# Attention's input in a Macaron block: both expert rows of a token summed by VectorE, the output bias summed later on GpSimd

## The chip, the cores and the metric

One core of one Trainium2 chip runs the kernel. The metric is device microseconds of one execution. Before the change three runs took 290.08, 288.76 and 292.3 us (median 290.08); one more execution was profiled.

## The reference, cut to what matters

The block is half an expert layer, attention, and half an expert layer again, each on a layer-normalised input and added to the residual x (4 sequences of 256 tokens, 512 channels, fp32):

```
def ffn(x):                                   # 8 experts, top 2, biases b_gate and b_e
    _, top_idx = top_k(x @ W_gate + b_gate, 2)
    y_all = relu(einsum('bsd,edh->bseh', x, W_e) + b_e)
    return take_along_axis(y_all, top_idx[..., None], axis=2).mean(axis=2)
def attn(x):                                  # one head of 128
    q, k, v = split(x @ Wqkv + bqkv)
    return softmax(q @ k.T / sqrt(128)) @ v @ Wo + bo
x = x + 0.5 * ffn(layernorm(x))
x = x + attn(layernorm(x))
x = x + 0.5 * ffn(layernorm(x))
```

What attention reads is therefore x plus two rows per token, one from each of its experts, already scaled by 0.25 (0.5 for the half layer, 0.5 for the mean). The output bias bo is added to x as well.

## The kernel before, in words

The 1024 tokens are 8 tiles of 128 (one token per partition, 512 channels along it). A batch is one sequence, so two tiles: batch b has tiles 2b and 2b+1. The tensor `x` holds all 8 tiles in SBUF and is updated in place.

In an expert layer tokens are sorted by expert into 23 tiles; GpSimd gathers their rows from HBM by indirect DMA, TensorE multiplies, and GpSimd scatters the results to `z_dram`, upper and lower row of each token apart. Attention then loads these rows back into `z_rows`, a ring of two slots (ZB = 2), each with both rows of one tile: `z[:, 0, :]` and `z[:, 1, :]`. Batch 0's four rows are loaded one by one (L376); tiles 2 to 7 come with one DMA each (L379), issued by SP when the tile two places ahead has been summed into x (semaphore `x_ffn`).

Every engine has its own program, written out by hand, and carries it out in that order; semaphores are the only tie between engines. Attention runs batch by batch:

- **VectorE** adds z to x (`add_z_batch`, L1167, with `add_z`, L1158), takes mean and variance (`moments`, L940), and, when GpSimd has made the reciprocal root (`deviations`, L435, instruction L442), normalises both tiles (`normalise`, L969, instruction L978, tensor `xn`). It also adds v's bias (L1176), takes the row maximum of the scores (L1218) and scales it to `nmax` (L1219), and adds attention's output to x (L1244), which also needs bo in x (semaphore `bo_added`).
- **GpSimd** sums, for tiles 2 to 7, both rows of z into the first (`sum_z`, L473, instruction L477, semaphore `z_summed`), so that VectorE adds one tensor per tile (L1165). For tiles 0 and 1 VectorE adds the rows one after the other (L1204 and L1162). GpSimd also adds bo to each tile of x, as soon as that tile is normalised (`add_bo`, L479, instruction L482).
- **TensorE** transposes xn (L698), projects to q and k (L822), then to v (L831), makes the scores (L840), transposes the probabilities (L848), mixes v (L856) and projects out (L866). Within batch b it also makes the transposes, q, k and v of batch b+1, and from batch 1 on the transposes ("g1") and the gate of the second expert layer for batch b-1.
- **ScalarE** copies results out of PSUM and takes the exponentials.

`norms` lists the order in which tiles are normalised, for attention ("att") and for the second layer ("g1"); `norm_no` is a tile's place in it and the count in the semaphore `xn_made`.

Of the kernel before, what the change touches and what calls it, by code (L numbers as in the profile page):

```python
# [6 lines left out]
ALU = mybir.AluOpType  # L7
# [11 lines left out]
def macaron_kernel(nc, x_in, w_qkv, b_qkv, w_o, b_o, w_gate, b_gate, w_e, b_e, out):  # L19
# [12 lines left out]

    B, S, H = x_in.shape
    E, _, HO = w_e.shape
    D = w_o.shape[0]
    T = B * S
    NT = T // P
    NC = H // P
    TB = S // P
# [17 lines left out]
    with ExitStack() as ctx:  # L57
        def sb(name, shape, dt=F32, at=ctx):
            return at.enter_context(nc.sbuf_tensor(name, shape, dt))
# [4 lines left out]
        def sem(name):  # L64
            return ctx.enter_context(nc.semaphore(name))
# [9 lines left out]
        ZB = 2  # L75
        MR = 8
        x = sb("x", [P, NT, H])
# [89 lines left out]
        def z_slot(i):  # L167

            return z_rows[:, i % ZB, :, :]
# [35 lines left out]
        dve_step = sem("dve_step")  # L205
# [3 lines left out]
        xn_made = sem("xn_made")  # L209
# [24 lines left out]
        z_in = [sem(f"z_loaded{s}") for s in range(ZB)]  # L234
        z_half_in = [[sem(f"z_half_loaded{k}_{i}") for i in range(NT // 2)] for k in range(TOP_K)]
        lower_added = sem("lower_added")
        z_first = [[sem(f"z_first{i}_{k}") for k in range(TOP_K)] for i in range(TB)]
        z_summed = sem("z_summed")
        x_ffn = sem("x_ffn")
        bo_added = sem("bo_added")  # L240
        qk_done = sem("qk_done")
# [28 lines left out]
        norm_no = {u: n for n, u in enumerate(norms)}  # L270
# [123 lines left out]
        def _(pool):  # L394
# [40 lines left out]
            def deviations(kind, b):  # L435

                n = norm_no[(kind, TB * b)]
                s = n % MR
                pool.wait_ge(var_made, n // TB + 1)
                if n >= MR:  # L440
                    pool.wait_ge(xn_made, n - MR + TB)
                pool.tensor_tensor(rstd[:, s:s + TB], var_eps[:, s:s + TB], neg_half[:], ALU.pow  # L442
                                   ).then_inc(rstd_made, 1)
# [26 lines left out]
                        gather(f, t + XG + 1)  # L470
                    scatter(f, t)

            def sum_z(i):  # L473

                pool.wait_ge(z_in[i % ZB], 16 * (i // ZB))
                z = z_slot(i)
                pool.tensor_tensor(z[:, 0, :], z[:, 0, :], z[:, 1, :], ALU.add).then_inc(z_summed, 1)  # L477

            def add_bo(b):  # L479
                for i in range(TB * b, TB * (b + 1)):  # L480
                    pool.wait_ge(xn_made, norm_no[("att", i)] + 1)
                    pool.tensor_tensor(x[:, i, :], x[:, i, :], bo_bc[:], ALU.add).then_inc(bo_added, 1)  # L482

            def attention_input(b):
                for i in range(TB * b, TB * (b + 1)):
                    sum_z(i)
                deviations("att", b)

            for b in range(B):
                deviations("g0", b)  # L490
            experts(0)
            pool.wait_ge(att_in, 16 * ATT_LOADS)
            deviations("att", 0)
            pool.wait_ge(xn_made, norm_no[("att", TB - 1)] + 1)
            attention_input(1)
            add_bo(0)
            add_bo(1)
            for b in range(B):
                if b + 2 < B:
                    for i in range(TB * (b + 2), TB * (b + 3)):  # L500
                        sum_z(i)
                if b:
                    deviations("g1", b - 1)
                if b + 2 < B:
                    deviations("att", b + 2)
                    add_bo(b + 2)
            deviations("g1", B - 1)
            experts(1)

# [417 lines left out]
        def _(dve):  # L927
            steps = [0]

            def step(ins):  # L930

                steps[0] += 1
                ins.then_inc(dve_step, 1)
                return steps[0]
# [5 lines left out]
            def moments(kind, b):  # L940

                n = norm_no[(kind, TB * b)]
                s = n % MR
                read = []
                for i in range(TB):
                    if kind == "g0":
                        dve.wait_ge(x_in_sem[TB * b + i], 16)
                    if (kind, b) == ("att", 0):
                        add_z(i)
                        dve.wait_ge(x_ffn, i + 1)  # L950
                    read.append(step(dve.bn_stats(stats[:, s + i, :], x[:, TB * b + i, :])))
                for i in range(TB):
                    dve.wait_ge(dve_step, read[i])
                    last = step(dve.bn_aggr(mv[:, s + i, :], stats[:, s + i, :]))
                dve.wait_ge(dve_step, last)
                if n >= MR:
                    dve.wait_ge(rstd_made, (n - MR) // TB + 1)
                dve.tensor_scalar(var_eps[:, s:s + TB], mv[:, s:s + TB, 1], EPS, None,  # L958
                                  ALU.add).then_inc(var_made, 1)
# [197 lines left out]

            def add_z(i):  # L1158

                if i < TB:  # L1160
                    dve.wait_ge(z_first[i][1], 16)
                    dve.tensor_tensor(x[:, i, :], x[:, i, :], z_slot(i)[:, 1, :], ALU.add).then_inc(x_ffn, 1)  # L1162
                else:
                    dve.wait_ge(z_summed, i - TB + 1)
                    dve.tensor_tensor(x[:, i, :], x[:, i, :], z_slot(i)[:, 0, :], ALU.add).then_inc(x_ffn, 1)  # L1165

            def add_z_batch(b):  # L1167
                for i in range(TB * b, TB * (b + 1)):
                    add_z(i)
                dve.wait_ge(x_ffn, TB * (b + 1))  # L1170

            def add_bv(b):
# [32 lines left out]
            moments("att", 0)  # L1205
            normalise("att", 0)
            add_z_batch(1)
            moments("att", 1)
            normalise("att", 1)
# [4 lines left out]
            for b in range(B):  # L1214
# [8 lines left out]
                if b + 2 < B:  # L1223
                    add_z_batch(b + 2)
# [15 lines left out]
                for q in range(TB):  # L1240
                    i = TB * b + q
# [48 lines left out]
```

## Time and profile before

| | us |
|---|---|
| median of three runs (288.76 to 292.3) | 290.08 |
| the profiled execution | 285.84 |
| its span, from first to last instruction | 284.0 |
| TensorE busy (PE; its weight loads, PEld, lie beside it) | 242.9 (86%) |
| VectorE busy (DVE) | 168.1 (59%) |
| GpSimd busy (POOL) | 127.6 (45%) |
| ScalarE busy (ACT) | 102.8 (36%) |
| GpSimd's sums of z (L477), 6 | 7.5 |
| GpSimd's sums of the bias (L482), 8 | 10.8 |
| VectorE's sums of z for tiles 2 to 7 (L1165), 6 | 6.0 |

Times within the execution count from the start of the span. Attention lies at about 121 to 178 us. "Busy" is the time in which an engine carries out instructions; idle time in front of an instruction is listed with what ended it. A granted clock of 1.00 is 2.4 GHz, 0.50 is 1.2 GHz.

### The profile page before, as it was taken

How to read it: one execution, taken by the hardware profiler on the slowest of the kernel's cores; microseconds unless marked ns; L12 is line 12 of the kernel's file. 1: busy time of each engine (PE TensorE's matmuls, PEld its weight loads, DVE VectorE, ACT ScalarE, POOL GpSimd, SP SyncE). 2: the span in 40 equal slices, each digit the busy share in tenths (PEclk: the TensorE clock that was granted, in tenths of full speed). 3: DMA queues.
4: the chain of work that ended last, by engine and by line, in shares of the span. 5: the costliest groups of instructions: out<-in, count | busy, mean ns of one | idle time of the engine just before them, and what ended most of it. 6: DMA issues, size and time to landing. Idle time of an engine off the chain costs nothing. (4 is left out here: it accounts for less than half of the span.)

```text
span 284.0 us, 4851 instructions
## 1 busy us (share of the span) xinstructions
PE 242.9 (86%) x1298; PEld 178.7 (63%) x1299; DVE 168.1 (59%) x404; ACT 102.8 (36%) x183; POOL 127.6 (45%) x141
## 2 busy tenths in 40 slices
PE   6677698989999999987999967559999999999730
PEld 2343266668888887566686934326888888887520
DVE  4589948976343444576888568872434344344770
ACT  1987425553333433112343442201343333333200
POOL 4200455765666563349464000024556666555150
PEclk9999999999999999999999999559999999999995
DMA  7999259993444365412401021104445434359891
GB/s 244 387 393 395 102 158 379 413 342 122 145 159 151 117 180 180 148 54 96 147 4 74 0 77 74 75 7 144 144 139 165 162 124 158 112 160 307 293 376 43
DMA packets 22787, 49.35 MB, mean 174 GB/s; under 512 B 4332, under 2 KB 4972, under 8 KB 22512
## 3 DMA queue, kind: packets, MB, share of 16 engines
q1 hardware_dynamic: 13712, 26.55, 25.9%
q0 software_dynamic: 7360, 20.46, 21.9%
q10 hardware_dynamic: 1696, 2.11, 2.0%
q8 instruction: 9, 0.15, 0.2%
q14 instruction: 10, 0.08, 0.1%
HBM read 34.42 MB, written 18.35 MB: 186 GB/s over the span
## 5 line engine op out<-in xcount | busy, mean ns | idle before, releaser
L457 POOL DMA_INDIRECT z_dram<-yrow,place x46 | 51.2, 1113 | 59.9 <-ACT yrow L587 42.1
L449 POOL DMA_INDIRECT xg<-xn_dram,tok x46 | 47.3, 1028 | 49.3 <-DVE tok L1109 32.9
L1120 DVE TENSOR_TENSOR xt_lo<-tp_ps,xt_hi 128x512 fp32r<-128x512 f32 x46 | 31.8, 691 | 56.1 <-ACT xt_hi L577 53.2
L587 ACT ACTIVATE yrow<-ypre 128x512 f32<-128x512 f32 x42 | 26.5, 632 | 84.7 <-DVE ypre L1128 46.5
L577 ACT ACTIVATE xt_hi<-tp_ps 128x512 fp32r<-128x512 f32 x46 | 26.8, 582 | 15.3 <-PE tp_ps L759 15.3
L759 PE MATMUL tp_ps<-ident,xg 128*128 128x128 f32 x184 | 27.9, 274 | 3.5 <-DMA xg<-xn_dram,tok 3.4
L782 PE MATMUL y_ps<-whi,xt_hi 128*128 x96 | 29.1, 425 | 1.7 <-ACT xt_hi L577 1.1
L759 PEld LDWEIGHTS tp_ps<-ident,xg 128*128 128x128 f32 x184 | 22.4, 140 | 11.4 <-DMA xg<-xn_dram,tok 6.1
L782 PE MATMUL qk_ps<-whi,xt_hi 128*128 x88 | 26.7, 425 | 0.6 <-issue 0.5
L782 PE MATMUL y_ps<-whi,xt_lo 128*128 x96 | 26.5, 398 | 0.0
L782 PE MATMUL y_ps<-wlo,xt_hi 128*128 x96 | 26.1, 393 | 0.0
L442 POOL TENSOR_TENSOR rstd<-var_eps,neg_half 128x2 f32<-128x2 f32 x12 | 8.4, 700 | 35.6 <-DVE var_eps L958 35.6
L782 PE MATMUL qk_ps<-whi,xt_lo 128*128 x88 | 24.1, 396 | 0.0
L782 PE MATMUL qk_ps<-wlo,xt_hi 128*128 x88 | 23.9, 393 | 0.0
L1128 DVE TENSOR_TENSOR ypre<-y_ps,be_bc 128x512 f32<-128x512 f32 x22 | 15.2, 691 | 11.8 <-PE y_ps L782 10.4
L685 PE MATMUL rk_ps<-ones 128*128 128x512 bf16 x63 | 19.3, 462 | 2.3 <-POOL neg_half L411 2.3
L782 PEld LDWEIGHTS y_ps<-wlo,xt_hi 128*128 128x128 f32 x96 | 18.1, 188 | 4.3
L782 PEld LDWEIGHTS y_ps<-whi,xt_hi 128*128 128x128 f32 x96 | 16.5, 190 | 6.4 <-issue 4.3
L782 PEld LDWEIGHTS y_ps<-whi,xt_lo 128*128 128x128 f32 x96 | 18.0, 189 | 4.1
L1128 DVE TENSOR_TENSOR ypre<-qk_ps,be_bc 128x512 f32<-128x512 f32 x20 | 13.8, 692 | 10.2 <-PE qk_ps L782 8.7
L305 DVE TENSOR_TENSOR wlo<-raw,whi 128x1024 fp32r<-128x1024 f32 x16 | 19.0, 1216 | 0.5 <-ACT whi L520 0.5
L782 PEld LDWEIGHTS qk_ps<-whi,xt_lo 128*128 128x128 f32 x88 | 16.6, 189 | 3.9
(130 smaller groups left out, 350.3 us busy)
## 6 DMA issues: line engine op xcount, KB each, us to landing
raw<-in_L_ffn_W_e_dram SPq DMA_DIRECT2D x16, 512.0 KB, 9.2
z_rows<-z_dram SPq DMA_DIRECT2D x6, 512.0 KB, 3.3
x<-in_L_attn_x_dram SPq DMA_DIRECT2D x8, 256.0 KB, 3.9
be_bc<-in_L_ffn_b_e_dram SPq DMA_DIRECT2D x2, 1024.0 KB, 12.6
xn_dram<-xn ACTq DMA_DIRECT2D x8, 256.0 KB, 2.0
whi<-z_dram SPq DMA_DIRECT2D x4, 512.0 KB, 4.6
wlo<-z_dram SPq DMA_DIRECT2D x4, 512.0 KB, 6.4
out_dram<-x SPq DMA_DIRECT2D x8, 256.0 KB, 2.8
```

The costliest lines, as they stand in the source:

```text
L305: eng.tensor_tensor(half(wlo, n), half(raw, n), half(whi, n).bitcast(F32), ALU.subtract).then_inc(done, 1)
L442: pool.tensor_tensor(rstd[:, s:s + TB], var_eps[:, s:s + TB], neg_half[:], ALU.pow).then_inc(rstd_made, 1)
L449: pool.indirect_dma_start(out=xg[:, t % XG, :], out_offset=None, in_=xn_dram[f][:, :], in_offset=bass.IndirectOffsetOnAxis(ap=tok[:, t:t + ...
L457: pool.indirect_dma_start(out=z_dram[f][:, :], out_offset=bass.IndirectOffsetOnAxis(ap=place[:, t:t + 1], axis=0), in_=yrow[:, t % YB, :], ...
L577: act.activation(xt_hi[:, t % 2, :], tp_ps[(n0 + t) % 2][:], ACT.Copy).then_inc(tp_copied, 1)
L587: act.activation(yrow[:, t % YB, :], ypre[:, t % 2, :] if t < NY else y_ps[t % 2][:], ACT.Relu, scale=HALF_MEAN).then_inc(yrow_made, 1)
L685: pe.matmul(bank[:], ones[:], ones[:].unsqueeze(1).broadcast_to([P, 4, P]), start=True, stop=True)
L759: last = pe.transpose(tp_ps[(n0 + t) % 2][:, c * P:(c + 1) * P], xg[:, t % XG, c * P:(c + 1) * P], ident[:])
L782: last = pe.matmul(y_ps[t % 2][:], rows[:, t % 2, c * P:(c + 1) * P], w[:, bass.ds(e * WE + c * H, H)], start=(n == 0), stop=(rows is xt_l ...
L1120: dve.tensor_tensor(xt_lo[:, t % 2, :], tp_ps[(n0 + t) % 2][:], xt_hi[:, t % 2, :].bitcast(F32), ALU.subtract).then_inc(xt_made, 1)
L1128: dve.tensor_tensor(ypre[:, t % 2, :], y_ps[t % 2][:], be_bc[:, bass.ds(e * H, H)], ALU.add).then_inc(ypre_made, 1)
```

## The change

GpSimd's `sum_z` and the semaphore `z_summed` go. VectorE's `add_z_batch` adds for a batch of two tiles first both lower rows, each behind its load, and then both upper rows, each behind the lower one's end; a slot is counted as read (`x_ffn`) at the second sum. For tiles 0 and 1 nothing changes. GpSimd's `add_bo(b)` now waits once, for all normalised tiles of batch b+1 (for the last batch, of its own), and stands later in GpSimd's program: batch 0 behind the root of batch 1, batches 1 and 2 behind the root of the batch two ahead, and batch 3 behind the second layer's root for its batch 1.

```diff
--- before.py
+++ after.py
@@ -235,7 +235,6 @@
         z_half_in = [[sem(f"z_half_loaded{k}_{i}") for i in range(NT // 2)] for k in range(TOP_K)]
         lower_added = sem("lower_added")
         z_first = [[sem(f"z_first{i}_{k}") for k in range(TOP_K)] for i in range(TB)]
-        z_summed = sem("z_summed")
         x_ffn = sem("x_ffn")
         bo_added = sem("bo_added")
         qk_done = sem("qk_done")
@@ -470,40 +469,27 @@
                         gather(f, t + XG + 1)
                     scatter(f, t)
 
-            def sum_z(i):
-
-                pool.wait_ge(z_in[i % ZB], 16 * (i // ZB))
-                z = z_slot(i)
-                pool.tensor_tensor(z[:, 0, :], z[:, 0, :], z[:, 1, :], ALU.add).then_inc(z_summed, 1)
-
             def add_bo(b):
+
+                pool.wait_ge(xn_made, norm_no[("att", min(TB * (b + 2), NT) - 1)] + 1)
                 for i in range(TB * b, TB * (b + 1)):
-                    pool.wait_ge(xn_made, norm_no[("att", i)] + 1)
                     pool.tensor_tensor(x[:, i, :], x[:, i, :], bo_bc[:], ALU.add).then_inc(bo_added, 1)
-
-            def attention_input(b):
-                for i in range(TB * b, TB * (b + 1)):
-                    sum_z(i)
-                deviations("att", b)
 
             for b in range(B):
                 deviations("g0", b)
             experts(0)
             pool.wait_ge(att_in, 16 * ATT_LOADS)
             deviations("att", 0)
-            pool.wait_ge(xn_made, norm_no[("att", TB - 1)] + 1)
-            attention_input(1)
+            deviations("att", 1)
             add_bo(0)
-            add_bo(1)
             for b in range(B):
-                if b + 2 < B:
-                    for i in range(TB * (b + 2), TB * (b + 3)):
-                        sum_z(i)
                 if b:
                     deviations("g1", b - 1)
                 if b + 2 < B:
                     deviations("att", b + 2)
-                    add_bo(b + 2)
+                    add_bo(b + 1)
+                if b + 2 == B:
+                    add_bo(B - 1)
             deviations("g1", B - 1)
             experts(1)
 
@@ -1157,16 +1143,18 @@
 
             def add_z(i):
 
-                if i < TB:
-                    dve.wait_ge(z_first[i][1], 16)
+                dve.wait_ge(z_first[i][1], 16)
+                dve.tensor_tensor(x[:, i, :], x[:, i, :], z_slot(i)[:, 1, :], ALU.add).then_inc(x_ffn, 1)
+
+            def add_z_batch(b):
+                tiles = range(TB * b, TB * (b + 1))
+                lower = []
+                for i in tiles:
+                    dve.wait_ge(z_in[i % ZB], 16 * (i // ZB))
+                    lower.append(step(dve.tensor_tensor(x[:, i, :], x[:, i, :], z_slot(i)[:, 0, :], ALU.add)))
+                for i, done in zip(tiles, lower):
+                    dve.wait_ge(dve_step, done)
                     dve.tensor_tensor(x[:, i, :], x[:, i, :], z_slot(i)[:, 1, :], ALU.add).then_inc(x_ffn, 1)
-                else:
-                    dve.wait_ge(z_summed, i - TB + 1)
-                    dve.tensor_tensor(x[:, i, :], x[:, i, :], z_slot(i)[:, 0, :], ALU.add).then_inc(x_ffn, 1)
-
-            def add_z_batch(b):
-                for i in range(TB * b, TB * (b + 1)):
-                    add_z(i)
                 dve.wait_ge(x_ffn, TB * (b + 1))
 
             def add_bv(b):
```

On VectorE, from the normalisation of batch 0 (`xn`) to that of batch 1; first as it was, then as it is:

```order
L978 TENSOR_SCALAR xn<-x,mv,rstd 128x512 [waits rstd_made,xn_stored0,tp_full]
L978 TENSOR_SCALAR xn<-x,mv,rstd 128x512 [waits rstd_made,xn_stored1,tp_full]
L1165 TENSOR_TENSOR x<-x,z_rows 128x512 [waits z_summed] x2
L951 BN_STATS stats<-x 128x6 [waits x_ffn]
L951 BN_STATS stats<-x 128x6
L954 BN_AGGR mv<-stats 128x2 [waits dve_step] x2
L958 TENSOR_SCALAR var_eps<-mv 128x2 [waits rstd_made,dve_step]
L978 TENSOR_SCALAR xn<-x,mv,rstd 128x512 [waits rstd_made,xn_stored2,tp_full]
L978 TENSOR_SCALAR xn<-x,mv,rstd 128x512 [waits rstd_made,xn_stored3,tp_full]
```

```order
L964 TENSOR_SCALAR xn<-x,mv,rstd 128x512 [waits rstd_made,xn_stored0,tp_full]
L964 TENSOR_SCALAR xn<-x,mv,rstd 128x512 [waits rstd_made,xn_stored1,tp_full]
L1154 TENSOR_TENSOR x<-x,z_rows 128x512 [waits z_loaded0]
L1154 TENSOR_TENSOR x<-x,z_rows 128x512 [waits z_loaded1]
L1157 TENSOR_TENSOR x<-x,z_rows 128x512 [waits dve_step] x2
L937 BN_STATS stats<-x 128x6 [waits x_ffn]
L937 BN_STATS stats<-x 128x6
L940 BN_AGGR mv<-stats 128x2 [waits dve_step] x2
L944 TENSOR_SCALAR var_eps<-mv 128x2 [waits rstd_made,dve_step]
L964 TENSOR_SCALAR xn<-x,mv,rstd 128x512 [waits rstd_made,xn_stored2,tp_full]
L964 TENSOR_SCALAR xn<-x,mv,rstd 128x512 [waits rstd_made,xn_stored3,tp_full]
```

The wait for GpSimd's sums is replaced by the waits for the two loads, and four sums stand where there were two.

On VectorE, behind the score maximum of batch 1: from the variance of the second layer's batch 0 (normalised into slots 2 and 3 of `xn`) to the first normalised tile of attention's batch 3 (slot 0); before, then now:

```order
L958 TENSOR_SCALAR var_eps<-mv 128x2 [waits rstd_made,dve_step]
L1165 TENSOR_TENSOR x<-x,z_rows 128x512 [waits z_summed] x2
L978 TENSOR_SCALAR xn<-x,mv,rstd 128x512 [waits xn_stored2,rstd_made,tp_full,x_ffn]
L978 TENSOR_SCALAR xn<-x,mv,rstd 128x512 [waits rstd_made,xn_stored3,tp_full]
L951 BN_STATS stats<-x 128x6 x2
L954 BN_AGGR mv<-stats 128x2 [waits dve_step] x2
L958 TENSOR_SCALAR var_eps<-mv 128x2 [waits rstd_made,dve_step]
L1176 TENSOR_TENSOR v<-v_ps,bv_bc 128x256 [waits ot_done,v_done]
L978 TENSOR_SCALAR xn<-x,mv,rstd 128x512 [waits rstd_made,xn_stored0,tp_full]
```

```order
L944 TENSOR_SCALAR var_eps<-mv 128x2 [waits rstd_made,dve_step]
L1154 TENSOR_TENSOR x<-x,z_rows 128x512 [waits z_loaded0]
L1154 TENSOR_TENSOR x<-x,z_rows 128x512 [waits z_loaded1]
L1157 TENSOR_TENSOR x<-x,z_rows 128x512 [waits dve_step] x2
L964 TENSOR_SCALAR xn<-x,mv,rstd 128x512 [waits xn_stored2,rstd_made,tp_full,x_ffn]
L964 TENSOR_SCALAR xn<-x,mv,rstd 128x512 [waits rstd_made,xn_stored3,tp_full]
L937 BN_STATS stats<-x 128x6 x2
L940 BN_AGGR mv<-stats 128x2 [waits dve_step] x2
L944 TENSOR_SCALAR var_eps<-mv 128x2 [waits rstd_made,dve_step]
L1164 TENSOR_TENSOR v<-v_ps,bv_bc 128x256 [waits ot_done,v_done]
L964 TENSOR_SCALAR xn<-x,mv,rstd 128x512 [waits rstd_made,xn_stored0,tp_full]
```

Here too two more sums stand ahead of both normalisations; nothing else moved.

On GpSimd, from the root of attention's batch 1 (`rstd`; right in front of it stood two more sums over `z_rows`) to the bias of batch 3; before, then now:

```order
L442 TENSOR_TENSOR rstd<-var_eps,neg_half 128x2 [waits xn_made,var_made]
L482 TENSOR_TENSOR x<-x,bo_bc 128x512 [waits xn_made] x4
L477 TENSOR_TENSOR z_rows<-z_rows 128x512 [waits z_loaded0]
L477 TENSOR_TENSOR z_rows<-z_rows 128x512 [waits z_loaded1]
L442 TENSOR_TENSOR rstd<-var_eps,neg_half 128x2 [waits xn_made,var_made]
L482 TENSOR_TENSOR x<-x,bo_bc 128x512 [waits xn_made] x2
L477 TENSOR_TENSOR z_rows<-z_rows 128x512 [waits z_loaded0]
L477 TENSOR_TENSOR z_rows<-z_rows 128x512 [waits z_loaded1]
L442 TENSOR_TENSOR rstd<-var_eps,neg_half 128x2 [waits xn_made,var_made] x2
L482 TENSOR_TENSOR x<-x,bo_bc 128x512 [waits xn_made] x2
L442 TENSOR_TENSOR rstd<-var_eps,neg_half 128x2 [waits xn_made,var_made] x3
```

```order
L441 TENSOR_TENSOR rstd<-var_eps,neg_half 128x2 [waits xn_made,var_made]
L476 TENSOR_TENSOR x<-x,bo_bc 128x512 [waits xn_made]
L476 TENSOR_TENSOR x<-x,bo_bc 128x512
L441 TENSOR_TENSOR rstd<-var_eps,neg_half 128x2 [waits xn_made,var_made]
L476 TENSOR_TENSOR x<-x,bo_bc 128x512 [waits xn_made]
L476 TENSOR_TENSOR x<-x,bo_bc 128x512
L441 TENSOR_TENSOR rstd<-var_eps,neg_half 128x2 [waits xn_made,var_made] x2
L476 TENSOR_TENSOR x<-x,bo_bc 128x512 [waits xn_made]
L476 TENSOR_TENSOR x<-x,bo_bc 128x512
L441 TENSOR_TENSOR rstd<-var_eps,neg_half 128x2 [waits xn_made,var_made]
L476 TENSOR_TENSOR x<-x,bo_bc 128x512 [waits xn_made]
L476 TENSOR_TENSOR x<-x,bo_bc 128x512
```

The six sums over `z_rows` are gone; each pair of bias sums waits once, the first pair (batch 0) stands alone behind batch 1's root, and the last pair (batch 3) stands behind one more root than before.

## Rows read from the trace of the kernel before

**Rows 1.** Busy time by stretch: us, count, granted clock (PEclk), DMA share, GB/s.

```profile
core 0: us, PE busy (x) PEld busy (x) DVE busy (x) ACT busy (x) POOL busy (x), PEclk, DMA share, GB/s
142.00:153.00 11.00, 11.00 (x65) 8.92 (x63) 9.20 (x21) 4.91 (x12) 5.25 (x6) 1.00 0.13 50
...
166.00:178.00 12.00, 7.34 (x53) 4.03 (x51) 9.47 (x36) 3.93 (x10) 1.38 (x2) 1.00 0.12 45
178.00:190.00 12.00, 6.33 (x54) 3.56 (x55) 10.53 (x56) 2.27 (x4) 0.35 (x1) 0.53 0.12 44
```

**Rows 2.** TensorE in time: start, us, operation, count, idle before.

```profile
127.31 1.95 PE L831 MATMUL v_ps<-wqkv,xt_att 128*128 128x128 f32 x16
...
130.07 0.65 PE L698 MATMUL tp_ps<-ident,xn 128*128 128x128 f32 x4 [0.81 <-DVE xn L978]
131.48 0.65 PE L698 MATMUL tp_ps<-ident,xn 128*128 128x128 f32 x4 [0.76 <-DVE xn L978]
...
132.88 3.72 PE L822 MATMUL qk_ps<-xt_att,wqkv 128*128 128x256 f32 x16
...
141.13 1.02 PE L866 MATMUL qk_ps<-wo,prob 128*128 128x512 f32 x2
141.99 1.04 PE L698 MATMUL tp_ps<-ident,xn 128*128 128x128 f32 x8
...
143.82 3.72 PE L822 MATMUL qk_ps<-xt_att,wqkv 128*128 128x256 f32 x16
...
153.07 1.11 PE L698 MATMUL tp_ps<-ident,xn 128*128 128x128 f32 x8
...
162.41 1.04 PE L698 MATMUL tp_ps<-ident,xn 128*128 128x128 f32 x8
```

**Rows 3.** VectorE in time, 105 to 200, same columns.

```profile
121.25 1.00 DVE L978 TENSOR_SCALAR xn<-x,mv,rstd 128x512 f32<-128x512 f32 x2 [3.79 <-POOL rstd L442]
123.64 2.34 DVE L1165 TENSOR_TENSOR x<-x,z_rows 128x512 f32<-128x512 f32 x2 [1.39 <-POOL z_rows L477]
...
128.63 2.79 DVE L978 TENSOR_SCALAR xn<-x,mv,rstd 128x512 f32<-128x512 f32 x2 [0.92 <-POOL rstd L442]
...
133.77 1.26 DVE L1219 TENSOR_SCALAR nmax<-smax 128x2 f32<-128x2 f32 x1
...
140.04 1.00 DVE L978 TENSOR_SCALAR xn<-x,mv,rstd 128x512 f32<-128x512 f32 x2 [0.59 <-POOL rstd L442]
...
144.66 1.23 DVE L1219 TENSOR_SCALAR nmax<-smax 128x2 f32<-128x2 f32 x1
...
147.60 1.31 DVE L1165 TENSOR_TENSOR x<-x,z_rows 128x512 f32<-128x512 f32 x2
...
152.47 1.00 DVE L978 TENSOR_SCALAR xn<-x,mv,rstd 128x512 f32<-128x512 f32 x2 [0.57 <-POOL rstd L442]
...
155.81 0.17 DVE L1219 TENSOR_SCALAR nmax<-smax 128x2 f32<-128x2 f32 x1
...
158.51 1.00 DVE L978 TENSOR_SCALAR xn<-x,mv,rstd 128x512 f32<-128x512 f32 x2 [0.92 <-POOL rstd L442]
```

**Rows 4.** GpSimd in time, 105 to 200, same columns.

```profile
122.33 2.50 POOL L477 TENSOR_TENSOR z_rows<-z_rows 128x512 f32<-128x512 f32 x2 [1.22 <-DVE xn L978]
...
128.47 5.31 POOL L482 TENSOR_TENSOR x<-x,bo_bc 128x512 f32<-128x512 f32 x4
...
143.37 2.49 POOL L477 TENSOR_TENSOR z_rows<-z_rows 128x512 f32<-128x512 f32 x2
147.57 0.70 POOL L442 TENSOR_TENSOR rstd<-var_eps,neg_half 128x2 f32<-128x2 f32 x1 [1.71 <-DVE var_eps L958]
```

**Rows 5.** DMA issues, 105 to 160: count, KB each, median us to landing.

```profile
z_rows<-z_dram SPq DMA_DIRECT2D x6, 512.0 KB, 3.3
```

**Rows 6.** TensorE in time, with the lower granted clock.

```profile
178.30 1.66 PE L698 MATMUL tp_ps<-ident,xn 128*128 128x128 f32 x8 [1.83 <-DVE xn L978]
...
180.71 1.08 PE L711 MATMUL g_ps<-xt_gate,wg 128*32 128x256 f32 x8
```

## The prediction

> **What bounds the kernel now.** I read first the busy time by stretch, to see which engine is full in which stage; then TensorE's instructions in order of time through attention, to see where it stops and for whom; then VectorE's and GpSimd's for the same microseconds, because the change moves work between these two.
>
> The program is two expert layers with attention between them. Only attention (about 121 to 178 us of the span) is touched. In it TensorE is the full engine for most of the time: 11.00 of 11.00 us busy from 142 to 153, at a granted clock of 1.00 (2.4 GHz) [rows 1]. From 166 to 178 it is busy for 7.34 of 12 us only, because there the work of the last batch goes from engine to engine. So a microsecond saved ahead of 166 reaches the end only if it lets TensorE go on sooner.
>
> TensorE does stop at the start. It ends the values of batch 0 at 129.26 (127.31 + 1.95), then waits 0.81 us for the first normalised tile of batch 1 and another 0.76 us for the second; batch 1's projection to q and k starts at 132.88 [rows 2]. The tiles are late because VectorE is held up beside GpSimd. Its two sums of batch 1 take 2.34 us, while the pair at 147.60 takes 1.31; its two normalisations at 128.63 take 2.79 us, while those at 152.47 take 1.00; nmax, an instruction over 2 columns, takes 1.26 and 1.23 us at 133.77 and 144.66, and 0.17 at 155.81 [rows 3]. Beside each slow one GpSimd is at work: the sum of both rows of z from 122.33, the bias sums from 128.47 to 133.78, the sums of z from 143.37 to 145.86 [rows 4].
>
> **The change part by part.** GpSimd loses six z sums, some 1.25 us each (2.49 for two) [rows 4]. VectorE gets six more sums: it adds four tensors for a batch of two tiles instead of two. The trace has no four in a row. Two independent ones take 1.31 [rows 3], so I take 2.62 for four. Less than that there is little to be had, since each pair's overlap is already in its 1.31; the upper bound is one free and one held pair, 1.31 + 2.34 = 3.65. I keep 2.62, since GpSimd is idle beside them, as follows.
>
> *Batch 1.* VectorE ends batch 0's normalisation at 122.25 (121.25 + 1.00) and so far waits 1.39 us for GpSimd's first sum [rows 3]. Now it starts at once: 122.25 + 2.62 = 124.87, where it ended at 125.98 before. From there to the normalisation it took 2.65 us (128.63 - 125.98: moments, then the root on GpSimd), so the first normalisation starts at 127.52. The bias of batch 0 now waits for batch 1's normalised tiles, so GpSimd is idle beside them: 1.00 us for both, done by 128.52 instead of 131.42 (128.63 + 2.79). TensorE is then the later one. It may go on some 0.16 us ahead of the modelled end of its last group (141.99 against 141.13 + 1.02), at 129.10; from the transposes to the projection it needs 1.83 us without waits (141.99 to 143.82) [rows 2]. So the projection starts at 130.93 instead of 132.88: **1.95 us gained**. It is all that TensorE's row can give: VectorE could be half a microsecond later and nothing would change; at the upper bound for the sums, 1.03 us later, some 0.4 us of it would go.
>
> *Batch 2.* nmax loses its hold (1.26 to 0.17), the sums go from 2.34 to 2.62: VectorE's work is 0.81 us shorter. It was done at 141.04, 0.95 us ahead of TensorE's 141.99 [rows 2, 3], and has some 1.7 us in hand now. Nothing gained, nothing lost.
>
> *Batch 3.* Here there is no slack: both tiles took 1.00 us from 152.47 and TensorE took the first at 153.07, just behind it [rows 2, 3]. nmax at 144.66 gets back to 0.17, which is 1.06 less, since the z sums that held it are gone; the four sums cost 2.62 instead of 1.31. Net +0.25 us on the way to this tile, and TensorE waits for it: **0.25 us lost** (1.28 at the upper bound).
>
> *The bias.* It is now summed for a batch only behind the normalisation of the next. Batch 0's runs from 128.5 to 131.2 (5.31 us for four [rows 4], 2.66 for two); nmax, which follows TensorE's scores, comes at 133.77 - 1.95 = 131.8, when GpSimd is idle. Batch 1's runs behind the tiles of batch 2, from about 138.3 (141.04 - 1.95 - 0.81) to 140.9, ahead of nmax at 144.66 - 1.95 = 142.7. Batch 2's takes the place that batch 3's had; it may start 0.4 us later, as it waits for both tiles, and then holds the third nmax by up to 0.4 us; that is hidden behind 3.72 us of projection [rows 2]. Batch 3's comes to a new place, behind the root for the second layer's batch 1, so it runs beside the normalisation at 158.51: I price that as the pair at 128.63, 2.79 for 1.00, or +1.79 us. TensorE takes these tiles at 162.41, 2.90 us after their end [rows 2, 3], so it is nothing unless that slack is gone. A bias is read only by the output of its own batch, which is a batch later; no new wait there. On GpSimd's queue the waiting bias stands ahead of the roots for the second layer; VectorE makes the tiles that it waits for before it makes those roots' input, so nothing new is late.
>
> *The loads of z* are issued when a slot's second sum is counted. The first such sum of batch 1 now ends near 124.2 (122.25 and three quarters of 2.62), the second at 124.87, and a load lands 3.3 us after its issue [rows 5], so both by 128.2; VectorE wants them behind nmax, at about 132. SP's queue is otherwise unmoved.
>
> One rule speaks against the change. The Trainium skill, SBUF — State Buffer, section "SBUF: two separate sides", says that VectorE and GpSimd share a port pair under an exclusive lock, held for a whole instruction, and that a VectorE instruction with two SBUF inputs must take it too. The slow sums and normalisations agree. By it GpSimd's root at 147.57, 0.70 us long, should hold a sum that starts beside it until 148.27; the pair at 147.60 took 1.31 us all the same [rows 3, 4], so the trace does not show that for this small instruction. By the rule the batch 3 chain would lose 0.67 us more (1.03 us gained in all), by the row nothing.
>
> **Sum.** 1.95 - 0.25 = 1.70 us. Everything behind batch 3 follows from TensorE's scores and shifts with them. The profiled execution took 285.84 us (span 284.0); it would take 284.1. The median of the three timed runs is 290.08, 4.2 us above the profiled one, in work that I cannot see; I take the same 1.70 off: **288.4 us**.
>
> **Rivals.**
>
> (a) VectorE sets the pace in batch 3: a hold by GpSimd stays on nmax (the bias of batch 1 comes late) or comes onto the sums. With the old hold on nmax the chain to batch 3's tiles is 1.31 us longer than now (0.25 + 1.06), so 0.64 of the 1.95 is left: 289.4. The upper bound for the sums gives about the same (1.28 lost), the hold by the root 289.1. For it: no slack at that point. Against: that bias ends 1.8 us ahead of nmax by the sum above. Chance 0.19.
>
> (b) The gain is hidden: the gap at 129 to 131 closes, but the batches that follow give all of it back. 290.1. For it: a wait of 1.95 us instead of 0.25 at batch 3 would do. Against: VectorE's work ahead of that point grows by 0.25 only. Chance 0.09.
>
> (c) Slower, by the clock. The clock fell to 1.2 GHz at about 178, after TensorE had been busy for 7.34 of 12 us; mean 0.53 from 178 to 190 [rows 1]. If the fall comes as early as the thin stretch itself begins, 166 in the old time, TensorE's work there costs more: a group of eight transposes took 1.66 us at the low clock and 1.04 at the high one [rows 2, 6], a factor of 1.6, so at most 0.6 x 7.34 = 4.4 us. Less the gain: +2.7, or 292.8. It decides from the point where the fall comes more than 4.6 us earlier (1.7 of 4.4, of 12 us). Against: the stretch is the same as before, and TensorE in front of it is busier, not idler. Chance 0.06. The Trainium skill, TensorE: Matmul & The Clock Gate, "What's actually happening", says that activity lifts the throttle, which by itself would move the fall the other way.
>
> (d) The fall does not come, or later. The transposes at 178.30 get 0.62 us back and the gate at 180.71, by the same factor, 0.40 [rows 6]. Gain 2.7 in all: 287.4. Chance 0.11.
>
> **Numbers.** The forecast has 0.55, (a) 0.19, (b) 0.09, (c) 0.06, (d) 0.11. The cases (d), forecast, (a) and (b) span 287.4 to 290.1. The runs of one kernel spread from 1.3 below to 2.2 above their median, and the profiled execution lies further below still; so the range goes from 285.2 (2.2 under (d)) to 291.4 (1.3 over (b)), with most of (c) left out. A change of 2%, 5.8 us, is about what a measurement of this kernel can tell from none, and no case moves the time by half of that. Faster by over 2% needs the spread of runs on top of (d), 0.05; slower by over 2% needs it on top of (c), 0.02; within 2%, 0.93.
>
> **What would show it.** Right: VectorE's four sums of batch 1 start with no wait behind the normalisation and take 2.5 to 2.8 us; the two normalisations of batch 1 take 1.0; TensorE goes from batch 0's values to batch 1's transposes without a wait; nmax takes 0.17 us in batches 0 and 1; at batch 3's transposes a wait of some 0.3 us; normalisations of about 2.8 us in the second layer's batch 1, with TensorE still running behind them. Wrong: a wait of a microsecond or more at batch 3's transposes, VectorE's sums held by GpSimd's root, or a granted clock below 1.00 ahead of the last batch's output.

## The result, and the profile after

| | before | changed | ratio, 95% interval |
|---|---|---|---|
| first comparison, median | 289.42 us (4 runs) | 284.88 us (4 runs, 284.22 to 286.03) | 0.9881 [0.9833, 0.9929] |
| measured anew, median | 288.48 us (35 runs) | 287.05 us (12 runs, 284.61 to 288.54) | 0.9961 [0.9926, 0.9995] |
| profiled execution | 285.84 us | 284.29 us | |
| its span | 284.0 us | 282.5 us | |

The change makes the kernel a little faster, by 0.4 to 1.2% as the two comparisons have it, and so by less than 2%. The forecast was a ratio of 1 - 1.70/290.08 = 0.9941. The first median lies 0.3 us below the range given (285.2), the second inside it. Runs over 1.5% above the fastest of their kernel are left out of every mean here. In the second comparison the changed kernel's mean is 286.66 us (12 runs, standard error 0.38) and that of the kernel before 288.28 (30 runs, 0.21): 1.6 us less. With the four runs of the first comparison the changed kernel's mean is 286.25 (16 runs, 0.35): 2.0 us less.

A difference of 2 us can't be read from two spans, since the part that the change doesn't touch moves by as much. In the execution profiled after, attention began 1.75 us later than before (the first transposes at 123.64 against 121.89), while the second layer's expert work and the end took some 1.6 us less. What can be read is the time from one place in TensorE's program to another:

| us on TensorE | before | changed | changed, again |
|---|---|---|---|
| attention's first transposes to those of batch 3 | 31.18 | 29.22 | 29.22 |
| batch 3's to the last transposes for the second layer | 25.23 | 25.17 | 25.18 |
| these to the second layer's first product | 16.20 | 16.54 | 16.22 |

The first row holds the change: 1.96 us, the same in both traces. With the second row it is 2.02 us over attention. The kernel before starts the first row here:

```profile
121.89 1.06 PE L698 MATMUL tp_ps<-ident,xn 128*128 128x128 f32 x8 [0.90 <-issue]
```

TensorE of the changed kernel in order of time; the columns are start, us, engine, line, operation, count, and the idle time before. It answers to [rows 2]:

```profile
123.64 1.07 PE L684 MATMUL tp_ps<-ident,xn 128*128 128x128 f32 x8 [0.89 <-issue]
...
129.06 1.95 PE L817 MATMUL v_ps<-wqkv,xt_att 128*128 128x128 f32 x16
130.84 1.04 PE L684 MATMUL tp_ps<-ident,xn 128*128 128x128 f32 x8
...
132.68 3.72 PE L808 MATMUL qk_ps<-xt_att,wqkv 128*128 128x256 f32 x16
...
152.86 1.04 PE L684 MATMUL tp_ps<-ident,xn 128*128 128x128 f32 x8
...
178.03 1.97 PE L684 MATMUL tp_ps<-ident,xn 128*128 128x128 f32 x8 [1.86 <-DVE xn L964]
```

Batch 1's transposes stood as two groups of four with 0.81 and 0.76 us of waiting. Now they are one group of eight and no wait stands in front of it: it starts 0.17 us before the modelled end of the values (129.06 + 1.95 = 131.01). The projection starts at 132.68 instead of 132.88, with a beginning 1.75 us later, so 1.95 us earlier within attention. Batch 3's transposes have no wait either.

VectorE, which answers to [rows 3]:

```profile
122.99 1.00 DVE L964 TENSOR_SCALAR xn<-x,mv,rstd 128x512 f32<-128x512 f32 x2 [3.79 <-POOL rstd L441]
123.91 1.29 DVE L1154 TENSOR_TENSOR x<-x,z_rows 128x512 f32<-128x512 f32 x2
125.11 1.28 DVE L1157 TENSOR_TENSOR x<-x,z_rows 128x512 f32<-128x512 f32 x2
...
129.04 1.00 DVE L964 TENSOR_SCALAR xn<-x,mv,rstd 128x512 f32<-128x512 f32 x2 [0.91 <-POOL rstd L441]
...
143.72 0.69 DVE L1206 TENSOR_REDUCE smax<-sp_ps 128x2 f32<-128x512 f32 x1 [0.91 <-PE sp_ps L826]
144.45 0.17 DVE L1207 TENSOR_SCALAR nmax<-smax 128x2 f32<-128x2 f32 x1
...
146.06 0.17 DVE L944 TENSOR_SCALAR var_eps<-mv 128x2 f32<-128x2 f32 x1
146.13 1.28 DVE L1154 TENSOR_TENSOR x<-x,z_rows 128x512 f32<-128x512 f32 x2
147.34 1.29 DVE L1157 TENSOR_TENSOR x<-x,z_rows 128x512 f32<-128x512 f32 x2
148.66 1.00 DVE L964 TENSOR_SCALAR xn<-x,mv,rstd 128x512 f32<-128x512 f32 x2
...
152.19 1.00 DVE L964 TENSOR_SCALAR xn<-x,mv,rstd 128x512 f32<-128x512 f32 x2 [0.57 <-POOL rstd L441]
...
155.53 0.27 DVE L1207 TENSOR_SCALAR nmax<-smax 128x2 f32<-128x2 f32 x1
...
158.33 2.79 DVE L964 TENSOR_SCALAR xn<-x,mv,rstd 128x512 f32<-128x512 f32 x2 [0.92 <-POOL rstd L441]
```

The four sums of batch 1 follow the normalisation at once and take 2.48 us (123.91 to 126.39). The normalisations of batch 1 take 1.00 us where they took 2.79, and nmax in batch 1 takes 0.17 where it took 1.23. The held normalisation has moved to 158.33, 2.79 us, where TensorE runs on until 162.13.

GpSimd, which answers to [rows 4]. It has no sums of z, and its bias sums stand behind the tiles of the batch that follows:

```profile
130.13 2.50 POOL L476 TENSOR_TENSOR x<-x,bo_bc 128x512 f32<-128x512 f32 x2 [1.22 <-DVE xn L964]
140.08 2.49 POOL L476 TENSOR_TENSOR x<-x,bo_bc 128x512 f32<-128x512 f32 x2 [1.48 <-DVE xn L964]
146.31 1.07 POOL L441 TENSOR_TENSOR rstd<-var_eps,neg_half 128x2 f32<-128x2 f32 x1 [3.74 <-DVE var_eps L944]
153.27 2.51 POOL L476 TENSOR_TENSOR x<-x,bo_bc 128x512 f32<-128x512 f32 x2 [1.22 <-DVE xn L964]
158.16 2.67 POOL L476 TENSOR_TENSOR x<-x,bo_bc 128x512 f32<-128x512 f32 x2
```

Busy time by stretch, which answers to [rows 1] (us, busy time and count of PE, PEld, DVE, ACT, POOL, granted clock, DMA share, GB/s):

```profile
142.00:153.00 11.00, 11.00 (x66) 8.93 (x65) 9.32 (x22) 4.90 (x12) 2.33 (x3) 1.00 0.13 50
166.00:178.00 12.00, 7.06 (x52) 4.00 (x51) 9.72 (x36) 3.92 (x10) 1.39 (x2) 1.00 0.12 45
178.00:190.00 12.00, 6.59 (x54) 3.90 (x55) 10.25 (x55) 2.27 (x4) 0.30 (x1) 0.50 0.12 44
```

GpSimd's busy time from 142 to 153 fell from 5.25 to 2.33 us, VectorE's rose by 0.12 only: what it took over it gets back in instructions that are no longer held. TensorE was full there and is full now. The clock falls in the last batch's thin stretch as before, to 0.50 from 178 on.

### The profile page after: what moved, and what is told of

Its sections match the earlier page's. It is cut to its first block and busy times, and to the rows that moved or that the text cites. A ratio compares the mean times of both kernels' runs of the same rounds, so it can differ in the third digit from the quotient of the medians.

```text
span 282.5 us, 4850 instructions
## 1 busy us (share of the span) xinstructions
PE 242.9 (86%) x1298; PEld 179.9 (64%) x1299; DVE 167.5 (59%) x410; ACT 102.7 (36%) x183; POOL 118.7 (42%) x135
## 5 line engine op out<-in xcount | busy, mean ns | idle before, releaser
L456 POOL DMA_INDIRECT z_dram<-yrow,place x46 | 50.0, 1087 | 61.5 <-ACT yrow L573 44.1
L768 PE MATMUL y_ps<-whi,xt_lo 128*128 x96 | 27.1, 405 | 0.0
L768 PE MATMUL y_ps<-wlo,xt_hi 128*128 x96 | 26.8, 402 | 0.0
L1114 DVE TENSOR_TENSOR ypre<-y_ps,be_bc 128x512 f32<-128x512 f32 x22 | 15.2, 691 | 11.9 <-PE y_ps L768 9.8
L768 PEld LDWEIGHTS qk_ps<-wlo,xt_hi 128*128 128x128 f32 x88 | 16.6, 189 | 3.9
```

The lines of the kernel that those rows point to most:

```text
L456: pool.indirect_dma_start(out=z_dram[f][:, :], out_offset=bass.IndirectOffsetOnAxis(ap=place[:, t:t + 1], axis=0), in_=yrow[:, t % YB, :], ...
L768: last = pe.matmul(y_ps[t % 2][:], rows[:, t % 2, c * P:(c + 1) * P], w[:, bass.ds(e * WE + c * H, H)], start=(n == 0), stop=(rows is xt_l ...
L1114: dve.tensor_tensor(ypre[:, t % 2, :], y_ps[t % 2][:], be_bc[:, bass.ds(e * H, H)], ALU.add).then_inc(ypre_made, 1)
```

## The experiments

The theory: the gain is the wait at batch 1's transposes, made of two causes (GpSimd's first sum is late, and its bias sums hold the normalisations), and batch 3 costs nothing. The rivals: it comes from one part alone; batch 3 sets the pace; the change gives something back through the clock.

**The changed kernel again** (no edit).

> The whole change, timed anew beside the kernel before. Theory: what is gained lies between TensorE's first transposes of attention and its last ones (56.41 us before, 54.39 after in the two traces, 2.02 less), and the rest of the 3.4 to 4.5 us between the medians is spread of the expert layers' loads and of the end: ratio about 0.993, this stretch again 54.4. Rival: the change also shortens something outside attention, by 1.4 us or more: ratio 0.988 again.

Measured: ratio 0.9961 [0.9926, 0.9995]; 29.22 us to batch 3 and 54.40 over attention, against 54.39 in the first trace. The theory held: the stretch is as long as before, and the interval leaves out 0.988. The stretch repeats to 0.01 us while the median moves by 2 us between two sets of runs, so the sizes below are taken from stretches.

**The sums alone.** VectorE sums both rows, the bias is added where it was before:

```diff
             def add_bo(b):
-                pool.wait_ge(xn_made, norm_no[("att", min(TB * (b + 2), NT) - 1)] + 1)
                 for i in range(TB * b, TB * (b + 1)):
+                    pool.wait_ge(xn_made, norm_no[("att", i)] + 1)
...
             add_bo(0)
+            add_bo(1)
...
-                    add_bo(b + 1)
-                if b + 2 == B:
-                    add_bo(B - 1)
+                    add_bo(b + 2)
```

> One part alone: VectorE sums both rows, GpSimd's bias sums stay where they were (batches 0 and 1 at once, behind batch 1's root). Theory (the normalisation of batch 1 is held by the bias beside it): the sums end 1.1 us sooner, both normalisations of batch 1 still take 2.8, so TensorE's second group of batch 1's transposes comes 1.2 us sooner than before, not 2.0; the stretch from attention's first to its last transposes is 55.2. Rival (it is the z sums on GpSimd that cost): 54.4, all of the gain.

Measured: ratio 0.9974 [0.9937, 1.0012]; 29.84 us to batch 3, so 1.34 of the 1.96 us. GpSimd, VectorE and TensorE at batch 1 in that kernel, in order of time:

```profile
127.86 5.31 POOL L475 TENSOR_TENSOR x<-x,bo_bc 128x512 f32<-128x512 f32 x4
128.02 2.80 DVE L962 TENSOR_SCALAR xn<-x,mv,rstd 128x512 f32<-128x512 f32 x2 [0.91 <-POOL rstd L441]
...
129.81 0.60 PE L682 MATMUL tp_ps<-ident,xn 128*128 128x128 f32 x4
130.87 0.66 PE L682 MATMUL tp_ps<-ident,xn 128*128 128x128 f32 x4 [0.46 <-DVE xn L962]
```

The bias sums run from 127.86 and the normalisations beside them take 2.80 us, so the second tile is late by 0.46 us. The theory held (1.34 us where 1.2 was put). From batch 3 on this execution lost what it had: 26.53 us instead of 25.2, since the clock fell at 169.4 already; so the whole stretch over attention is 56.37 us and not the 55.2 expected.

**The bias alone.** GpSimd still sums z, the bias waits for the next batch's tiles (the kernel before with the new `add_bo` and its places):

```diff
             def add_bo(b):
+                pool.wait_ge(xn_made, norm_no[("att", min(TB * (b + 2), NT) - 1)] + 1)
                 for i in range(TB * b, TB * (b + 1)):
-                    pool.wait_ge(xn_made, norm_no[("att", i)] + 1)
...
             add_bo(0)
-            add_bo(1)
...
-                    add_bo(b + 2)
+                    add_bo(b + 1)
+                if b + 2 == B:
+                    add_bo(B - 1)
```

> The other part alone: GpSimd still sums both rows of z, and the bias goes behind the normalisation of the next batch. Theory: VectorE's sums of batch 1 still end 1.2 us late, but both normalisations take 1.00, so the first tile comes at the moment when TensorE is free: stretch 54.5 to 54.7, nearly all of the gain. Rival (the z sums cost): 56.1, as good as none.

Measured: ratio 0.9943 [0.9898, 0.9987]; 29.42 us to batch 3, so 1.76 us. VectorE and TensorE in that kernel:

```profile
125.07 2.34 DVE L1167 TENSOR_TENSOR x<-x,z_rows 128x512 f32<-128x512 f32 x2 [1.38 <-POOL z_rows L477]
...
130.07 1.00 DVE L980 TENSOR_SCALAR xn<-x,mv,rstd 128x512 f32<-128x512 f32 x2 [0.92 <-POOL rstd L442]
...
130.68 1.11 PE L700 MATMUL tp_ps<-ident,xn 128*128 128x128 f32 x8
```

VectorE still waits 1.38 us for GpSimd and its sums still take 2.34, but the normalisations take 1.00, and TensorE takes the tiles without a listed wait, 0.2 us later than with the whole change: its projection starts 9.24 us behind attention's first transposes and not 9.04. The theory held up to batch 3; from there on this execution too lost by an early fall of the clock (27.91 us, 57.33 over attention). So the two parts don't add up (1.34 + 1.76 is well over 1.96): each alone closes most of one wait, and behind its end TensorE is the later one. Of the parts, moving the bias is worth more.

**A bias sum beside VectorE's sums.** This brings about the mishap that rival (a) feared: batch 0's bias is summed ahead of batch 1's root, while VectorE sums z.

```diff
             deviations("att", 0)
+            pool.wait_ge(xn_made, norm_no[("att", TB - 1)] + 1)
+            for i in range(TB):
+                pool.tensor_tensor(x[:, i, :], x[:, i, :], bo_bc[:], ALU.add).then_inc(bo_added, 1)
             deviations("att", 1)
-            add_bo(0)
```

> The whole change, but batch 0's bias stands ahead of batch 1's root on GpSimd, so it runs beside VectorE's four sums of batch 1. Theory (a two-input sum on VectorE and one on GpSimd exclude each other): the four sums take 2.5 + 2 x 1.26 = 5.0 us, TensorE waits some 1.3 us for batch 1, stretch 55.7. Rival (only the short forms, normalisation and nmax, are held): the sums take 2.5 us and the stretch is 54.4.

Measured: ratio 0.9958 [0.9915, 1.0001]; 29.22 us to batch 3, no cost. VectorE, GpSimd and TensorE in order of time:

```profile
125.37 1.29 DVE L1156 TENSOR_TENSOR x<-x,z_rows 128x512 f32<-128x512 f32 x2
125.53 4.69 POOL L485 TENSOR_TENSOR x<-x,bo_bc 128x512 f32<-128x512 f32 x2 [1.22 <-DVE xn L966]
126.57 1.29 DVE L1159 TENSOR_TENSOR x<-x,z_rows 128x512 f32<-128x512 f32 x2
...
129.43 0.82 DVE L946 TENSOR_SCALAR var_eps<-mv 128x2 f32<-128x2 f32 x1
...
131.16 1.00 DVE L966 TENSOR_SCALAR xn<-x,mv,rstd 128x512 f32<-128x512 f32 x2 [0.92 <-POOL rstd L441]
...
132.30 1.04 PE L686 MATMUL tp_ps<-ident,xn 128*128 128x128 f32 x8
```

The expectation of held sums missed. VectorE's first sum started 0.16 us ahead of GpSimd's, and all four took their free time; GpSimd's two took 4.69 us instead of 2.50. Only var_eps was held, 0.82 instead of 0.17, and with it batch 1's normalisation came 0.66 us later (6.71 us behind batch 0's, from 124.45 to 131.16, where the change alone has 6.05). TensorE took the tiles at 132.30, 1.14 us behind that start, without a wait; with the change alone it is 1.80, and in batch 3, where there is next to no slack, 0.67. So the delay went into slack. (From batch 3 on it is 27.92 us, by an early fall of the clock; over attention 57.14.)

**A fifth sum in batch 3**, to see how much slack VectorE has there:

```diff
+                if b == B - 1:
+                    step(dve.tensor_tensor(xg[:, 0, :], z_slot(0)[:, 0, :], z_slot(0)[:, 1, :], ALU.add))
                 for i, done in zip(tiles, lower):
```

> The whole change, and one sum more of the same size on VectorE among the four of batch 3 (into a buffer that nobody reads). It asks how much slack VectorE has there. Theory (the prediction's rival a: hardly any, 0.1 us): TensorE waits 0.5 us for batch 3's first tile, and from attention's first transposes to batch 3's it takes 29.7 us instead of 29.22. Rival (slack of over half a microsecond): 29.22.

Measured, one execution: 29.75 us to batch 3 instead of 29.22, and the wait is there, in TensorE's row:

```profile
155.74 1.11 PE L684 MATMUL tp_ps<-ident,xn 128*128 128x128 f32 x8 [0.37 <-DVE xn L964]
```

A sum of 0.6 us costs 0.53: the slack in batch 3 is about 0.1 us. The forecast was right that there is next to none; the change just fits.

**The kernel before, a second trace** (no edit).

> The kernel before, unchanged, for a second trace. Theory: from attention's first to batch 3's transposes 31.2 us again; the moment at which the clock falls behind 166 may be another one than in the first trace (178.3).

Measured: 290.0 us. To batch 3 it is 31.17 us, as in the first trace (31.18). From there to the last transposes it is 26.51 instead of 25.23, because the clock fell at 172.9, was back at 176.4, and fell again at 183.2. TensorE's first group behind the fall, which takes 1.13 us in the first trace, and then three stretches:

```profile
173.36 2.08 PE L856 MATMUL sp_ps<-pt,v 128*128 128x256 f32 x4 [0.69 <-ACT pt L667]
```

```profile
172.00:178.00 6.00, 5.31 (x22) 3.89 (x22) 3.81 (x21) 2.11 (x4) 0.69 (x1) 0.72 0.23 87
178.00:184.00 6.00, 3.74 (x31) 2.02 (x29) 4.88 (x18) 1.07 (x2) 0.69 (x1) 0.93 0.09 35
184.00:190.00 6.00, 2.66 (x27) 1.08 (x26) 5.43 (x37) 1.08 (x3) 0.00 (x0) 0.50 0.14 54
```

So the early fall that rival (c) feared from the change befalls the kernel before too. Over all eight traces without extra matmuls the clock first fell, behind 166, between 168.6 and 180.7. Counted from batch 3's transposes these moments lie in two places: 15.9 to 16.9 us behind them in four traces, about TensorE's two waits (1.84 and 0.69 us) behind the last batch's gate, and 24.9 to 25.6 us behind them in the other four, at its wait of some 1.85 us for the last transposes. A fall at the first place cost 1.3 to 2.75 us up to the last transposes. Three kernels with a part of the change (the sums alone, the bias alone, the bias beside the sums) had the fall at the first place in their one trace, the changed kernel in neither of its two, and the kernel before in one of two; that is too few to say that one of them has it more often.

**Filler matmuls in the thin stretch**, in the changed kernel and in the kernel before. They multiply the ones of the warm-up into a bank that nobody reads any more, where TensorE waits in the last batch:

```diff
+                if b == B - 1:
+                    pe.wait_ge(v_made, B)
+                    warm_up(8, v_ps)
...
+                if b == B - 1:
+                    warm_up(2, v_ps)
                 mix_v(b)
...
             gate(1, B - 2)
+            warm_up(2, v_ps)
             transpose_logits(1, B - 2)
-            warm_up(3, v_ps)
+            warm_up(10, v_ps)
             transpose_xn("g1", B - 1)
             count(1, B - 2)
             gate(1, B - 1)
+            warm_up(2, v_ps)
             transpose_logits(1, B - 1)
+            warm_up(4, v_ps)
             count(1, B - 1)
+            warm_up(13, v_ps)
```

> The whole change, and 41 instead of 3 matmuls of ones (128x512, results unused) in TensorE's waits from the last batch's gate to the token list, 0.21 us each at 2.4 GHz. Theory (the spread of executions in this stage is the clock, which falls at some moment of the thin stretch, and the early falls seen in three traces cost 1.4 to 2.7 us each): the granted clock stays at 1.00 from 166 to 192, from batch 3's transposes to the last group it takes 25.2 us as without an early fall, from there to the second layer's first product 14.5 to 15.0 us instead of 16.2, and the mean of the runs falls by 1.5 us or more below the change alone (286.3). Rival (the early falls are rare, the fillers overrun the waits): this part takes as long or longer, and the mean stays.

> The same fillers in the kernel before. With the clock held in both, what the change itself is worth shows without the falls. Theory: 2.0 us between the means of this kernel and of the change with fillers, as between their traces. Rival (the change gives part of its gain back by earlier falls of the clock, as its lower mean clock of 0.956 against 0.961 hints): with fillers in both the difference is 2.0, while without them it stays near 1.1.

Measured: up to the last transposes the trace with the change takes 25.17 us from batch 3, as expected, and from there to the first product 16.18, not 14.5 to 15.0. The times are, with the change, 0.9867 [0.9804, 0.993] of the kernel before, mean 285.42 us (5 runs, standard error 0.7); without it 0.9967 [0.9923, 1.001], mean 287.51 (10 runs, 0.4). The difference between them is 2.1 us with a standard error of 0.8; without the fillers it is 1.6 (0.4) within one comparison. So nothing speaks for a change that gives back through the clock, but these runs are too few to exclude it. Against the mean of the changed kernel (286.25, from other comparisons) the fillers brought 0.8 us, less than expected and no more than the error. They held the clock at 1.00 from 166 to 190 and then TensorE waited 2.12 us for the gather, and the clock was low for the second layer's first matmuls:

```profile
189.17 2.32 PE L671 MATMUL rk_ps<-ones 128*128 128x512 bf16 x10
193.61 1.05 PE L745 MATMUL tp_ps<-ident,xg 128*128 128x128 f32 x4 [2.12 <-DMA xg<-xn_dram,tok]
...
195.44 2.04 PE L768 MATMUL y_ps<-whi,xt_hi 128*128 x4
```

**The fillers, and a longer warm-up ahead of the second layer**, which closes that wait:

```diff
-        WARM = [16, 10]
+        WARM = [16, 18]
```

> The change with the fillers, and 18 instead of 10 matmuls of ones behind the token list, so that TensorE is busy until the first gathered rows land, some 5.1 us behind the token list. Theory: the clock stays at 1.00 up to the second layer's first product, its transposes take 0.66 instead of 1.05 and its first group 1.2 instead of 2.0; from the last group of transposes to the first product 14.9 to 15.2 us instead of 16.2, and the mean of the runs is 1 us below that of the fillers alone (285.4). Rival: the gather lands later too and takes the gain, 16.2 again.

Measured: 284.07 us median (6 runs, 283.51 to 285.87), mean 284.30, ratio to the kernel before 0.9853 [0.9799, 0.9906]. It is the version with the lowest mean. TensorE at the gather, and the two stretches:

```profile
187.16 4.04 PE L671 MATMUL rk_ps<-ones 128*128 128x512 bf16 x18
191.67 0.66 PE L745 MATMUL tp_ps<-ident,xg 128*128 128x128 f32 x4 [0.47 <-DMA xg<-xn_dram,tok]
...
193.10 1.19 PE L768 MATMUL y_ps<-whi,xt_hi 128*128 x4
```

```profile
166.00:178.00 12.00, 11.34 (x69) 6.12 (x68) 9.77 (x38) 3.93 (x10) 1.39 (x2) 1.00 0.12 45
178.00:190.00 12.00, 9.73 (x79) 4.42 (x78) 10.22 (x57) 2.16 (x4) 1.44 (x2) 1.00 0.12 46
```

The clock is 1.00 throughout, the transposes take 0.66 us instead of 1.05, the first product 1.19 instead of 2.04. The stretch from the last transposes to that product is 15.85 us, though, and not the 14.9 to 15.2 expected: with the clock at 1.00 all along it is only 0.4 to 0.7 us shorter than without fillers, so something other than TensorE's clock sets most of it. The gain over the changed kernel, 286.25 - 284.30 = 1.95 us between means taken in different comparisons, is more than the stretch shows; that the rest is the early falls that no longer occur fits the sizes above, but was not counted run by run.

## Why the prediction was right, step by step

**Batch 1, 1.95 us gained: right**, in place and size. VectorE's sums start without a wait, batch 1's normalisations take 1.00 us, TensorE goes on without a wait, and its projection is 1.95 us earlier within attention. The two part-kernels show that the step is one wait with two causes, as it was worked out, and that TensorE's row and not VectorE's sets what can be had.

**Batch 2, nothing: right.** TensorE goes from output to transposes without a listed wait.

**Batch 3, 0.25 us lost: did not occur.** It is the mis-sized term. Three rows of the kernel before, beside those of [rows 3]:

```profile
143.93 0.69 DVE L1218 TENSOR_REDUCE smax<-sp_ps 128x2 f32<-128x512 f32 x1 [0.91 <-PE sp_ps L840]
...
147.33 0.17 DVE L958 TENSOR_SCALAR var_eps<-mv 128x2 f32<-128x2 f32 x1
...
148.95 1.00 DVE L978 TENSOR_SCALAR xn<-x,mv,rstd 128x512 f32<-128x512 f32 x2
```

From the maximum of batch 1's scores to the normalised tiles of batch 3 VectorE took 8.54 us before (143.93 to 152.47) and takes 8.47 now (143.72 to 152.19). nmax is shorter by 1.06, as forecast. The four sums take 2.50 (146.13 to 147.34 + 1.29 = 148.63) where 2.62 was put. Up to the start of the next instruction they take 2.53 (146.13 to 148.66) where two took 1.35 (147.60 to 148.95), so they add 1.18 instead of 1.31: the second pair starts 1.21 us behind the first, before the 1.28 us of that are over. The remaining 0.20 is the gap in front of them: from the start of var_eps to the first sum it was 0.27 us before (147.33 to 147.60) and is 0.07 now (146.06 to 146.13). That gap is 0.27 with the bias alone moved and 0.07 with the sums alone moved, so it goes with GpSimd's sums of z and VectorE's wait for them; what in it takes the time was not shown. Hence -1.06 + 1.18 - 0.20 = -0.08, against the 0.07 measured, where the forecast put +0.25. TensorE shows it too: batch 3's transposes took 1.11 us and take 1.04, which is the 0.06 that the second row of the table adds. So it is 2.02 us over attention instead of 1.70. That there was hardly any slack at this point was right; that the sums would outweigh nmax was not.

**The bias: right.** Batch 0's and batch 1's sums end ahead of nmax; the third nmax is held by 0.1 us (0.27 at 155.53); the normalisations of the second layer's batch 1 take 2.79 us at 158.33 and nobody waits for them.

**The rule about the shared port.** No trace shows VectorE's sums held by GpSimd's root. In the changed kernel the sum starts at 146.13 and the root at 146.31, and the root takes 1.07 us instead of 0.70; the same 1.07 stands in every trace in which the sum starts first. That the sum held the root is what these rows suggest. The Trainium skill, SBUF — State Buffer, section "SBUF: two separate sides", says that whichever starts first gets the pair for the whole instruction; this trace agrees with 1.07. The pair at 147.60 before, 0.03 us behind the root and not held (1.31 us), does not agree with it, nor does the pair in the kernel with the bias alone moved, 0.02 us behind its root and 1.31 us long.

**Rival (c), a slower kernel by an earlier fall of the clock**, was right as a mechanism; as an effect of the change it is not shown. It costs 1.3 to 2.75 us where it occurs (4.4 was the bound), the kernel before has it too, and neither trace of the changed kernel does.

**The range** missed the first median by 0.3 us and holds the second. Its middle was taken off a median of three runs (290.08) that lies 1.8 us above the mean of the 30 runs measured later; between traces it is the fall of the clock and the first layer (84.7 to 88.9 us from its first product to attention's first transposes) that differ by as much. Of the 4.5 us between the medians of the first comparison the traces show 2.0 as the change's; the rest was not seen again in the second.

## What to carry to other kernels

Where two causes delay the same wait, find what is the later one once the wait is gone: either edit alone brought 1.3 to 1.8 us here and both together 1.96. Moving work to a busier engine was free, because on the other engine the same work had held it by as much: in batch 3 nmax by 1.06 us, in batch 1 the pair of sums by 1.03 (2.34 instead of 1.31). The normalisations' 1.79 us were the bias sums' doing and came back by moving those to another time. When the total moves by 2 us between executions, measure a change of 2 us from one instruction to another on the engine that is full, where it repeats to 0.01 us.

## What the runs showed of the hardware that was not expected

When VectorE's two-input sums follow each other without a gap and GpSimd has sums of the same size at the same time, VectorE keeps its pace (2.49 us for four) and GpSimd waits (4.69 instead of 2.50 for two); before, with GpSimd's sums running first, it was VectorE's that took 2.34 instead of 1.31.

TensorE's granted clock falls from 2.4 to 1.2 GHz at one of two places in executions of one kernel (at 172.9 and at 178.7 in two traces of the kernel before, 16.8 and 25.6 us behind batch 3's transposes). In the first trace TensorE was busy for 7.34 of the 12 us ahead of it (166 to 178), with no wait of more than 1.84 us. With the fillers and the longer warm-up it was busy for 11.34 of these 12 us and the clock did not fall. The Trainium skill, TensorE: Matmul & The Clock Gate, "What's actually happening", says that activity releases the throttle; the fillers agree, with 1.00 from 166 to 190 against 0.50 to 0.53 from 178 to 190 in the first traces of both kernels.
